# Order of stores at the start of the expert stage, and of results, roots and scatters at its end

## What is computed

```python
probs = softmax(flat @ gate_W)                      # flat: 2048 rows of 256
topk_w, topk_idx = top_k(probs, 2)                  # two experts a row
out = 0.5 * gelu(flat @ shared_W + shared_b)
for e in range(8):
    h = gelu(flat @ W1[e] + b1[e])                  # 256 -> 1024
    out = out + combine[:, e:e+1] * (h @ W2[e] + b2[e])   # 1024 -> 256
out = (out - mean) * rsqrt(var + 1e-5) * gamma + beta
return x + out
```

## Time and profile before

| | |
|---|---|
| median of 3 runs | 774.73 us (773.8 to 778.24) |
| profiled execution | 781.06 us |
| its span, first to last instruction | 779.2 us |
| PE busy | 720.6 us (92%) |
| DVE, ACT, POOL busy | 378.4, 436.3, 222.2 us |
| expert tiles on PE | from 502 to 766 us |

### The profile page before, as it was taken

How to read it: one execution, slowest core, us unless ns; L and a number is a source line. 1 busy time by engine, 2 the same in 40 slices (tenths; PEclk the granted TensorE clock), 3 DMA queues, 4 the chain that set the end, 5 groups by cost and what they waited for, 6 DMA issues and landing times.

```text
span 779.2 us, 20188 instructions
## 1 busy us (share of the span) xinstructions
PE 720.6 (92%) x7240; PEld 480.7 (62%) x7241; DVE 378.4 (49%) x1358; ACT 436.3 (56%) x772; POOL 222.2 (29%) x257
## 2 busy tenths in 40 slices
PE   4977999999999999998899898979999999999992
PEld 2434445464444444443454556778999999999991
DVE  5763221202044525348858456215665565565564
ACT  2746888988798989885557252233323333333320
POOL 2030050101000000020005135744554554554554
PEclk9999999999999999999999889999999999999997
DMA  9565958999021220304832455676666567677751
GB/s 208 147 223 185 283 144 260 275 338 319 11 84 42 65 84 22 104 3 125 264 117 75 130 176 173 197 249 212 181 220 213 187 219 249 215 226 258 232 171 57
DMA packets 91017, 135.19 MB, mean 173 GB/s; under 512 B 14558, under 2 KB 75755, under 8 KB 88602
## 3 DMA queue, kind: packets, MB, share of 16 engines
q1 hardware_dynamic: 82200, 117.71, 49.6%
q0 software_dynamic: 8736, 16.40, 6.0%
HBM read 96.13 MB, written 52.85 MB: 191 GB/s over the span
## 4 chain that ended last, share of the span: by engine, by line
PE 72%; DVE 9%; DMA 6%; ACT 6%; issue 3%; SPq 3%; POOL 1%; DVEq 0%; POOLq 0%; ACTq 0%
PE ps L2294 15%; PE ps L1951 15%; PE ps L2282 15%; PE ps L1928 13%; ACT arena L937 3%; DMA q_parts<-arena 2%; PE ps L2088 1%; DMA x_sb<-in_x 1%; PE ps L1910 1%; PE ps L1966 1%; PE ps L2004 1%; PE ps L2269 1%; SPq L616 1%; DMA k_parts<-arena 1%; PE ps L2164 1%
## 5 line engine op out<-in xcount | busy, mean ns | idle before, releaser
L937 ACT ACTIVATE arena<-ps 128x1024 f32<-128x1024 f32 x256 | 241.3, 1033 | 35.5 <-PE ps L1951 35.0
L1951 PE MATMUL ps<-arena 99*32 99x512 bf16 x2048 | 162.0, 387 | 4.4 <-issue 2.9
L1928 PE MATMUL ps<-arena 128*32 128x256 f32 x2048 | 159.6, 381 | 0.6 <-issue 0.6
L2282 PEld LDWEIGHTS ps<-arena 128*128 128x128 f32 x1120 | 130.3, 192 | 5.1 <-ACT arena L1048 1.8
L2282 PE MATMUL ps<-arena 128*128 128x128 f32 x1120 | 130.9, 275 | 2.7 <-issue 1.3
L2294 PE MATMUL ps<-arena,xh_tag 128*128 x560 | 128.0, 382 | 1.3 <-ACT xh_tag L1067 1.3
L2294 PEld LDWEIGHTS ps<-arena,xh_tag 128*128 128x128 f32 x560 | 104.8, 192 | 14.6 <-issue 1.5
L1048 ACT COPY arena<-ps 128x256 f32<-128x256 f32 x35 | 13.0, 372 | 163.6 <-PE ps L2269 158.9
L1928 PEld LDWEIGHTS ps<-arena 128*32 128x32 f32 x2048 | 65.9, 111 | 52.6 <-issue 3.4
L1951 PEld LDWEIGHTS ps<-arena 99*32 99x32 bf16 x2048 | 39.6, 95 | 71.1 <-ACT arena L937 50.0
L1067 ACT ACTIVATE xh_tag<-ps,arena 128x128 f32<-128x128 f32 x280 | 76.5, 392 | 6.8 <-PE ps L2282 6.8
(11 more groups left out here) (266 smaller groups left out, 882.2 us busy)
## 6 DMA issues: line engine op xcount, KB each, us to landing
arena<-in_L_ffn_W SPq DMA_DIRECT2D x43, 1024.0 KB, 8.8
rows_by_expert<-arena SPq DMA_DIRECT2D x9, 1965.0 KB, 15.8
arena<-q_parts SPq DMA_DIRECT2D x90, 128.0 KB, 2.6
row_parts<-arena SPq DMA_DIRECT2D x3, 2048.0 KB, 17.2
arena<-k_parts SPq DMA_DIRECT2D x42, 128.0 KB
q_parts<-arena SPq DMA_DIRECT2D x12, 384.0 KB, 2.6
arena<-rows_by_expert SPq DMA_DIRECT2D x35, 131.0 KB, 2.1
arena<-in_L_ffn_b SPq DMA_DIRECT2D x35, 128.0 KB
```

The lines of the kernel that those rows point to most:

```text
L937: nc.scalar.activation(probs_of(stage, h), ps[:, 2 * (u % 2):2 * (u % 2) + 2, :].rearrange("p a n -> p (a n)"), ACT.Exp, scale=float(D) ** ...
L1928: last = nc.tensor.matmul(ps[32 * h:32 * h + 32, 4 + half, at:at + 256], v_grp[n % 2][:, kt, h, :], probs_of(stage, h)[:, 256 * part:256 * ...
L1951: last = nc.tensor.matmul(ps[c:c + 32, 2 * (u % 2) + half, :], k_stk[buf][:, h, P * st + c:P * st + c + 32], q_stk[buf][:, h, 512 * half:5 ...
L2282: last = nc.tensor.matmul(ps[:, 4 * buf + half, P * c:P * (c + 1)], w1_buf[:, buf, k, at:at + P], xs_t[:, buf, k, :], start=(k == 0), stop ...
```

## The change

SP: the eight stores leave their place before `begin` and go into `start_sp`. After the load of the third tile's rows come the x part and base 1, then the third tile's W1, then bases 2 and 3, then the wait `parts_there` as before.

POOL: at the end `write_out(36)` goes ahead of `root(37)`.

DVE: the loop runs one round less, and that round is written out. In it `result(37)` moves from behind `normalised(35)` to its middle, behind `tags(38)`.

```diff
@@ start_sp
                 load_rows(slots_of(2 * k + 2), 0)
+                sp.wait_ge(x_last, 1)
+                store_part(3, 2, x_sb, row_out)
+                store_base(1)
+                e = expert(2 * k + 2)
                 sp.wait_ge(h_ps, 4 * k + 2)
-                load_w1(expert(2 * k + 2), 0)
+                load_w1(e, 0)
+                for ch in (2, 3):
+                    store_base(ch)
                 if k < MAYBE:
                     parts_there()
                     sp.sem_inc(may_read, 1)
@@ block.sync
                 load_b2(begin_with[j], j)
-            sp.wait_ge(x_last, 1)
-            store_part(3, 2, x_sb, row_out)
-            for ch in range(1, NT // CHUNK):
-                store_base(ch)
             begin(sp, run_flags(nc.sync), start_sp)
@@ block.gpsimd
             read_parts(FINAL)
+            write_out(FINAL - 2)
             root(FINAL - 1)
-            for s in (FINAL - 2, FINAL - 1):
-                write_out(s)
+            write_out(FINAL - 1)
             root(FINAL)
@@ block.vector
-            with dve.Fori(MAYBE, PAIRS) as i:
+            with dve.Fori(MAYBE, PAIRS - 1) as i:
                 round_dve(i)
-            result(1, FINAL - 1, 16 * (PAIRS + 1))
+            result(1, FINAL - 3, 16 * PAIRS)
+            normalised(0, FINAL - 4, 16 * PAIRS, between=lambda: tags(1, FINAL - 1))
+            result(0, FINAL - 2, 16 * (PAIRS + 1))
+
+            def last_but_one():
+                tags(0, FINAL)
+                result(1, FINAL - 1, 16 * (PAIRS + 1))
+
+            normalised(1, FINAL - 3, 16 * PAIRS, between=last_but_one)
             normalised(0, FINAL - 2, 16 * (PAIRS + 1))
             normalised(1, FINAL - 1, 16 * (PAIRS + 1), between=lambda: result(0, FINAL, 16 * (PAIRS + 2)))
             normalised(0, FINAL, 16 * (PAIRS + 2))
```

## The result

Before took 779.67 us (median of 22 runs), after 783.1 us (22 runs): ratio 1.0048, 95% interval 1.0028 to 1.0068. The change makes the kernel 3.7 us slower (2.2 to 5.3). The median of before stood at 774.73 us in the three runs that the prediction had; in 22 it is 5 us higher. The profiled execution of after took 788.2 us, its span is 786.4 us (before 781.06 and 779.2). It is the slowest of the 22, so its trace shows more of the loss, 7.2 us, than the medians do.

The account below looks back on a forecast made before the run. PE is fully busy mid-stage, so only the expert stage's two ends were taken to matter. Front 2.9 us plus tail 1.9 us gave 4.8 us off the median 774.73: 769.9 us, range 767.0 to 774.5.

Parts of the forecast that it names:

- Rows(6) hidden, the 3.30 us hole gone, L2(4) at full clock: Front: rows(6) issued at 504.8, landed before PE needs it; the 3.30 us PE hole goes; L2(4) takes 3.5 us.
- W1(6) lands 5.6 us after its issue: Front: W1(6), issued at 509.6 to 509.8, lands at 515.3, and L1(6) starts then instead of at 520.2.
- The bounds, 4.7 and 6.3: Front: W1 landing time, at least 4.7 us from bytes and bandwidth, at most 6.3 us from W1(6) in the old profile.
- `parts_there` passes at 517.0: Front: SP's wait for all 16 stores ends at 517.0, between 516.5 and 517.6, leaving a 1.7 us hole for rows(7).
- rival 3: Front: close holes bring the clock to 1.2 GHz or W1 takes 6.3 us; gain 3.2 or 1.5, about 772.3 us; chance 0.17.
- The 1.31 us hole at the jump kept: Front, L1(8) at the jump into the loop: hole stays 1.31 us, since the jump isn't touched.
- Scatter(4) in 3 us: Front, POOL: scatter(4) at 519.1, its released read 3.7 us later, rows(8) near 523.5; warned that tile 6's took over 7.
- the early steps: Tail: result(37) starts 1.29 us earlier, then scatter(37), read(37) and read(38) earlier too; 1.1 us gained so far.
- rival 2: Tail: POOL's 2.82 us gap moves ahead of root(37); gain 1.2 to 3.2 us, about 772.5 us; chance 0.18.
- B: The tail part, DVE's written-out round and POOL's order: gains 1.9 us, or 1.7 if the gap again follows root(37).
- Rival 4: Front, the slower side: the last store lands late, each us after 517.0 at parts_there delaying PE by one; chance 0.05.
- deciding point: Front: parts_there passing at 521.8, which is 517.0 + 4.8, decides for the whole; at 523.5 the time is 776.4 us.

Follow-up runs that it names:

- r_after: The changed kernel traced once more with no edit, one run: 782.07 us.
- e1_front: The kernel before with SP's part of the change alone, DVE and POOL as before: 784.57 us against 778.95, ratio 1.0077.
- e14_little_w1_6: e1_front with only an eighth of W1(6) loaded, all eight stores in place, so that tile's product is wrong: 781.5 us.
- r_before: The kernel before traced once more with no edit, one run: 775.18 us.
- e2_tail: The kernel before with the DVE and POOL parts of the change alone, SP as before: 779.14 us, ratio 1.0014.
- e6_rows_only: e1_front with only rows(6) ahead of the stores and W1(6) behind all eight: 778.46 us, ratio 1.0008 against before.
- e10_rows_dve: e6_rows_only with DVE's part of the change added and POOL's order of before: 778.9 us against 779.57, ratio 1.0005.
- e3_step_first: e1_front with rows(7) and W1(7) loaded ahead of the wait parts_there: 782.01 us, ratio 1.0022 against before.
- e7_no_bases: e1_front without the stores of bases 2 and 3, so part of the output is never written: 775.99 us, ratio 0.9967 against before.

## Why the prediction was wrong

The forecast was 769.9 us with a range to 774.5; measured 783.1. Of the 13.2 us between them 4.9 are the median of before, which three runs had put too low, 4.8 the gain that didn't come, and 3.4 the loss that did. Point by point, times from tile 4's transpose on (in before 502.05):

- **Rows(6) hidden, the 3.30 us hole gone, L2(4) at full clock: right.** Tile 6 at 9.1 us in every kernel with this order.
- **W1(6) lands 5.6 us after its issue: wrong, the first step that failed.** The bounds, 4.7 and 6.3, came from bare rates and from a W1 that was issued when the stores had landed. It took 8.9 us (7.9 and 8.3 in r_after and e1_front); without the four stores behind it, 6.9. With no stores beside it a W1 needs less than I took, not more: in the six traces with SP's order of before its last packet ends 4.4 to 4.5 us after the issue. So it is the term for the stores around it that was too small; "No row isolates a W1" was true of the rows, not of the trace's packets. W1(5) with its 7.1 us in a full queue was the nearer row, and I used it only to lean inside the bounds. L1(6) was predicted at 13.3 us and came at 15.9 (14.6, 14.8).
- **`parts_there` passes at 517.0, 14.9 us after the transpose: wrong.** It passed at 18.6, for the same reason from the other side: I charged the stores 3.1 us for the bytes of W1(6) and rows(6) ahead of them, and e14_little_w1_6 shows 3.9 us of the wait to come from W1(6). The mechanism named as next was right, its size was not: tile 7 predicted at 18.6 us, measured 22.4 (20.7, 21.1).
- **The clock: rival 3 named it**, and it fell in all three. In after the hole of 2.96 us brought L1(6) to 0.50 and cost 2.9 us; in e1_front and r_after two holes of 1.6 to 1.9 and 2.4 us brought L2(5) to 5.3 us.
- **The 1.31 us hole at the jump kept: the costliest error.** Tile 8 to tile 9 takes 15.5, 13.6 and 13.0 us in after, r_after and e1_front, 8.8 in before and 10.6 in r_before. Of the 6.7 us in after 3.8 are the hole and 2.8 L1(8) at the clock of 0.50. "Its cause isn't touched" was an argument about code, while PE's branch is a duration in the trace, 3.8 us that end just as L2(6) does: hidden with no cover to spare. And the cover of W1(8) and rows(8) that I worked out as 2.4 and 2.8 us said that the loads come in time, not what they now lie beside.
- **Scatter(4) in 3 us, with a warning of 7: 6.4**, so the warned case came.
- **Tail: the early steps right** (result(37) 1.56 us earlier, forecast 1.29; read(38) 1.3, forecast 1.0). **The sum was rival 2:** the gap stands ahead of root(37), and B is 0.6 us, not 1.9. Rival 2 gave 0.3; e1_front's tail of 22.0 against e2_tail's 21.3 gives 0.7.
- **Rival 4, the slower side, had 0.05.** The place was right, the point was not: `parts_there` passed at 18.6 us, below its deciding point of 19.75 (521.8), and the kernel is slower all the same, because the point assumed every other term of the sum. The failed steps are not independent: a late W1(6), late stores and a late scatter share one cause or follow one another, and I gave each a chance of its own. The longer jump comes with SP's new order too, but not by way of W1(6): it stood with that load cut (e14_little_w1_6).

## What to carry to other kernels

A load moved up among stores on the same queue is not in front of them: both slow down, so price it by the row of a load in a full queue, and price the stores' last waiter as well. Before a load is shifted, look at everything that now lies beside it, the taken branches too. Where several terms of a sum hang on the same queue, let them fail together in the range.

## What the runs showed that was not expected

- **W1 (1.05 MB) beside stores:** 5.3 us when issued behind all eight (e6_rows_only; 7.5 in e10_rows_dve, same order), 6.9 behind four stores of 256 KB, 7.9 to 8.9 between four and four, each time until PE starts on it. Its last packet ends 4.4 to 4.5 us after the issue where no store moves beside it. The Trainium skill, "DMA: Bandwidth & Descriptors", section "Anatomy of one DMA", gives by its fit, made with DMAs that GpSimd issued, an estimate of 4.4 us; the traces agree for a W1 without stores beside it, if the 0.4 us from its last packet to PE's start are allowed for.
- **A taken branch of PE** takes 3.4 to 6.6 us here, at one place of the program and on the same data. The Trainium skill, "Runtime: NRT & Kernel Launch", section "Instruction fetch mechanics", ties such a branch to a fetch over DMA; the traces agree with it, by the 16 KB packets under each branch and by the run with less traffic (5.24 against 6.44 us).
- **The clock** doesn't follow the length of the last hole alone: it held at 1.00 after 3.50 us (e6_rows_only) and 2.98 us (e3_step_first), and fell to 0.50 after 2.96 us (after) and after 2.25 us (e7_no_bases, L1(8) 5.33 us).
